# The tail of a two-layer graph network: edges in 171 pairs of tiles with a table of groups, against 90 units of four

## The chip, the cores and the metric

One core of one Trainium2 chip runs the whole program. The metric is the device time of one execution in microseconds. The kernel before took 3299.7 us (median of 3 runs, 3299.06 to 3302.92).

## The reference

1250 nodes with 768 features and 41250 edges (`src`, `dst`), each with one of 34 types. Two layers, each followed by a residual and a layer norm. The first is two attention convolutions and a projection. The second, which the change touches, is in short:

```python
seg = edge_type * n + dst
agg = segment_sum(x[src], seg); mean = agg / max(cnt, 1)
h1  = einsum('rni,rio->no', mean, W_rel) + x @ W_root + b_rgcn
out = segment_sum(h1 @ W_gcn, normalised over src, dst) + b_gcn
```

## The kernel before

**Edges.** The edges are sorted by destination into 10 groups ("buckets") of 128 nodes. One tile is 128 edges, one on each partition; a unit is UT = 4 tiles that belong to one group. UNITS = 90 units (ET = 360 tiles) hold any 41250 edges; places left over in a group's last unit are padding of weight 0. `dst_s`, `w_s` and `idx_y` have a column per tile: the destination in the group, the edge's weight 1/count and the row to gather. `unit_bucket` says which group a unit adds to.

**The relation products.** The kernel first multiplies by the weights, then gathers: for two halves of the output columns (CH = 384) and 17 pairs of relations each it runs steps of 35 products (seven combinations m1 to m7 of blocks, by five node tiles t; a product is nine f16 matmuls, lines 2501 to 2504). ACT evicts m1, m7, m6 and m3 (L1286), DVE adds m2, m5 and m4 (L1936), SP stores the rows to `y_half`. PE's order in a step is m1(0), m1(1), m7(0), m7(1), m6(0), m6(1), m2(0) and so on; m6(t) waits until ACT has copied m1(t). ACT's step begins with `used_high` for the weights of m4 (L1219), m1_out(0), `used_high` for m3, m1_out(1), m7_out(0), m7_out(1). While the second half's products run, the edges of the first half are aggregated beside them.

**The tail.** The edges of the second half are aggregated last, when all of `y_half` is stored. POOL gathers a tile at a time (`tail_gather`, L911, one indirect DMA of 128 rows of 384 floats), into 16 buffers, after `e_sum` says that the tile 16 before is used. DVE makes the weighted one-hot of each tile (`tail_onehot`, L1910, scalars straight from `dst_s` and `w_s`), PE multiplies it by the gathered rows (`tail_sum`, L2490, fp32, two records per tile) and sums the four tiles of a unit in one bank of PSUM; two banks take turns, and unit u waits until unit u-2 is added. DVE reads the unit's group into a register and adds the bank to that group's rows (`edge_add`, L1922). ACT copies the indices of the unit six ahead (`tail_index`, `next_index`, L1267) after unit u is summed. Beside the units run, in an order that is written out:
- units 0 to 37 (ROOT_UNITS): the 35 products of the root weight, one and a half per unit, done by unit 20; then ten tiles of `cT` (640 KB each, L765), one every 1.5 units from unit 21 on, three buffers; ACT takes the high half (`c_split`), DVE the rest (`c_rest`, L1980) two units later, and the load of tile c+3 waits for the rest of tile c;
- units 38 to 87: 25 pieces of the first half's graph product and of its product by W_gcn (L2735 to L2748), one piece after every second unit; units 88 and 89 have none.

When all units are added (`e_added`), the second half's graph product, the last product and the layer norm follow (`FINAL`), from there to the end of the program.

**Two earlier places.** At the start DVE works out the groups' units from their counts (L1592 to L1601, each operation waits for the one before it: `after`). Between the two attention layers DVE runs `spread_pads` (L1804) and then waits for the second layer.

```python
            def edge_add(q, i, m, c, roots=0):
                V, place, _ = unit(q, i, m, c)
                b = dve.value_load(unit_bucket[0:1, bass.ds(i * m + c, 1)], min_val=0, max_val=NT - 1)
                o = bass.ds(b * CH, CH)
                dve.wait_ge(e_sum, V * UT + 2 * UT)
                dve.wait_ge(e_added, V + 2)
```

Of the kernel before, what the change touches and what calls it, by code (L numbers as in the profile page):

```python
# [5 lines left out]
ALU = mybir.AluOpType  # L6
# [9 lines left out]
def cdiv(a, b):  # L16
    return -(-a // b)


def program(nc, x, src, dst, etype, norm_g, norm_b, W1, a_src1, a_dst1, b1, W2, a_src2, a_dst2, b2,  # L20
# [24 lines left out]
    CW = N + R  # L45
    TURN, EYES = 6, 2
# [7 lines left out]
    with ctx:  # L54
# [71 lines left out]
        rel_inv = src_s[:, 0:NT * R].rearrange("p (b r) -> p b r", r=R)  # L126
        epsc = sb("epsc", [P, 1], F32)
# [402 lines left out]
        REST = UNITS - ROOT_UNITS  # L530
        assert REST == 2 * len(PIECES) + 2

# [32 lines left out]
        def tail_slot(i, m, c, t):  # L565

            units = len(tail_rows) // UT
            assert m % units == 0 or isinstance(i, int)
            k = c % units * UT + t
            before = UNITS // 2 + W_USES[0] if k < 2 * UT else W_USES[1]  # L570
            return k, (g_loaded + tail_loaded)[k], i * (m // units) + (c // units + before + 1 + EYES_READ[k])
# [13 lines left out]
        def _(sp):  # L585
# [175 lines left out]
            for c in range(NT):  # L761
                sp.wait_ge(e_added, UNITS + CT_AT[c] + 2)
# [6 lines left out]
            sp.wait_ge(e_added, HALVES * UNITS + 2)  # L769
# [11 lines left out]
        def _(pool):  # L781
# [120 lines left out]
            def tail_gather(i, m, c):  # L902

                V = i * m + (c + (HALVES - 1) * UNITS)
                pool.wait_ge(idx_next, V + 1)
                for t in range(UT):
# [3 lines left out]
                    k, loaded, _ = tail_slot(i, m, c, t)  # L910
                    nc.gpsimd.indirect_dma_start(  # L911
                        out=tail_rows[k], out_offset=None, in_=y_dram[HALVES - 1],
                        in_offset=bass.IndirectOffsetOnAxis(ap=idx_now[:, c % IDXB, t:t + 1], axis=0)).then_inc(loaded, 16)
# [77 lines left out]
            with pool.Fori(0, UNITS // (2 * IDXB)) as i:  # L991
                for c in range(2 * IDXB):
                    tail_gather(i, 2 * IDXB, c)
            for c in range(UNITS // (2 * IDXB) * 2 * IDXB, UNITS):
                tail_gather(0, UNITS, c)
# [12 lines left out]
        def _(act):  # L1008
# [485 lines left out]
            def tail_index(i, m, c):  # L1494

                act.wait_ge(e_sum, i * (m * UT) + ((HALVES - 1) * UNITS + c + 2) * UT)
                next_index(i * m + (c + IDXB), c)

            for u in range(ROOT_UNITS):
                for m, t in root_slots(u):  # L1500
                    root_out(m, t)
                tail_index(0, UNITS, u)
                for m, t in root_slots(u - 1) if u else ():
                    if m == 3:
                        root_high(t)
                if u in CT_SPLIT:
                    c_split(CT_SPLIT.index(u))
            for m in range(len(PIECES)):
                for c in (ROOT_UNITS + 2 * m, ROOT_UNITS + 2 * m + 1):
                    if c + IDXB < UNITS:  # L1510
                        tail_index(0, UNITS, c)
                piece_out(m)
            for c in range(ROOT_UNITS + 2 * len(PIECES), UNITS - IDXB):
                tail_index(0, UNITS, c)

            act.wait_ge(e_added, HALVES * UNITS + 2)
# [10 lines left out]
        def _(dve):  # L1527
# [66 lines left out]
            fcnt, uend, ustart, base = (small[:, i * NT:(i + 1) * NT] for i in range(1, 5))  # L1594
            after(nc.vector.tensor_scalar(smalli[:, :], bank[6][:, NT:2 * NT], float(UE - 1), None, ALU.add))
# [206 lines left out]

            def spread_pads():
# [11 lines left out]
            spread_pads()  # L1815
            dve.wait_ge(s2_ready, NT)
# [87 lines left out]
            def tail_onehot(i, m, c):  # L1904

                V, place, _ = unit(HALVES - 1, i, m, c)
                for t in range(UT):
                    at = bass.ds((i * m + c) * UT + t, 1)
                    dve.wait_ge(e_sum, V * UT + (t + 1 + UT - 2 * UT))
                    nc.vector.tensor_scalar(tail_oh[place * UT + t], iota[:, 0:P], dst_s[:, at], w_s[:, at],  # L1910
                                            ALU.is_equal, ALU.mult).then_inc(e_oh, 1)

# [227 lines left out]
            def root_add(t, u):  # L2140
# [4 lines left out]
                dve.wait_ge(e_added, UNITS + u + 3)  # L2145
# [12 lines left out]
            tail_onehot(0, UNITS, 0)  # L2158
# [6 lines left out]
            for u in range(ROOT_UNITS):  # L2165
                tail_onehot(0, UNITS, u + 1)
                for m, t in root_slots(u):
                    root_out(m, t)
                edge_add(HALVES - 1, 0, UNITS, u, roots)
# [10 lines left out]
            first, last = ROOT_UNITS, HALVES - 1  # L2180
            with dve.Fori(0, REST // 2 - 1) as i:
                tail_onehot(i, 2, first + 1)
                edge_add(last, i, 2, first, roots)
                tail_onehot(i, 2, first + 2)
                edge_add(last, i, 2, first + 1, roots)
            tail_onehot(0, 2, UNITS - 1)
            edge_add(last, 0, 2, UNITS - 2, roots)
            edge_add(last, 0, 2, UNITS - 1, roots)

            dve.wait_ge(e_added, HALVES * UNITS + 2)  # L2190
# [18 lines left out]
        def _(pe):  # L2209
# [271 lines left out]
            def tail_sum(i, m, c):  # L2481

                V, place, _ = unit(HALVES - 1, i, m, c)
                acc = bank[SUMS + place][:, 0:CH]
                pe.wait_ge(e_added, V + 1)
                for t in range(UT):
                    k, loaded, uses = tail_slot(i, m, c, t)
                    pe.wait_ge(e_oh, (i * m + c) * UT + (t + 1))
                    pe.wait_ge(loaded, uses * 16)
                    nc.tensor.matmul(acc, tail_oh[place * UT + t], tail_rows[k], start=(t == 0), stop=(t == UT - 1))\  # L2490
                        .then_inc(e_sum, 1)
# [222 lines left out]
            for u in range(ROOT_UNITS):  # L2714
                for m, t in root_slots(u):
                    MAKE[m](STEPS - 1, t)
                tail_sum(0, UNITS, u)
# [35 lines left out]
            for m, (kind, j, cs) in enumerate(PIECES):  # L2753
                tail_sum(0, UNITS, ROOT_UNITS + 2 * m)
                tail_sum(0, UNITS, ROOT_UNITS + 2 * m + 1)
# [9 lines left out]
            for u in range(ROOT_UNITS + 2 * len(PIECES), UNITS):  # L2765
                tail_sum(0, UNITS, u)

            pe.wait_ge(e_added, HALVES * UNITS + 2)
# [36 lines left out]
```

## Time and profile before

| what | value |
|---|---|
| median of 3 runs | 3299.7 us |
| the profiled execution's own time | 3300.49 us |
| its span, first to last instruction | 3298.8 us |
| mean granted TensorE clock | 0.982 |
| the tail, first gather to last add | 2735.15 to 3201.13 us |
| what follows the tail | 97.7 us |

Times in the rows are in us from the start of the span. PE is TensorE's matmuls, PEld its weight loads, DVE VectorE, ACT ScalarE, POOL GpSimd, SP the engine that issues the loads and stores. "Idle before" is the time an engine stood still before an instruction, with the instruction that ended it; "issue" is waiting for nothing that the profile shows, the engine's own sequencer included. Matmuls overlap in the records, so their means are longer than their spacing.

### The profile page before, as it was taken

The page shows a single profiled execution, that of the slowest core. Times are in us where ns is not written, and L with a number is a line of the kernel's source. Part 1 is how long each engine was busy: PE and PEld are TensorE (multiplying, and loading weights), DVE is VectorE, ACT ScalarE, POOL GpSimd, SP SyncE. Part 2 cuts the span into 40 slices and gives each one's busy share as a digit, 9 for nine tenths or more (in the row PEclk, how much of TensorE's full clock was granted, in tenths as well). Part 3 has the DMA queues.
Part 4 walks back from the last instruction along what each step waited for, and adds up shares of the span by engine and source line. Part 5 has one row for each costly group of instructions (what it writes and reads, how often), then busy time and mean ns, then how long its engine had stood idle before and what let it go on. Part 6 is the DMA issues. An engine that isn't in the chain of part 4 may idle for free.

```text
span 3298.8 us, 59790 instructions
## 1 busy us (share of the span) xinstructions
PE 3128.9 (95%) x17442; PEld 1963.0 (60%) x17442; DVE 2259.3 (68%) x4621; ACT 1431.7 (43%) x2534; POOL 1822.0 (55%) x1510
## 2 busy tenths in 40 slices
PE   6979998988999999999999999999999999879998
PEld 4545558967566666666666666666666665434545
DVE  8989988959855564555646788787887865443335
ACT  3746647636534344343444554554555532110010
POOL 3767700001666666766514566566665636777763
PEclk9999999998999999999999999999999999999999
DMA  4047722021343333333325555565565634665542
GB/s 135 2 157 214 213 75 84 1 91 44 118 137 109 128 133 101 132 112 129 134 105 175 168 195 177 175 200 171 171 202 166 196 126 145 191 215 158 157 139 78
DMA packets 241012, 458.34 MB, mean 139 GB/s; under 512 B 40228, under 2 KB 180387, under 8 KB 240918
## 3 DMA queue, kind: packets, MB, share of 16 engines
q1 hardware_dynamic: 169248, 271.42, 23.7%
q0 software_dynamic: 71280, 185.21, 19.8%
q8 instruction: 54, 0.88, 0.1%
q10 hardware_dynamic: 390, 0.50, 0.1%
q14 instruction: 40, 0.33, 0.0%
HBM read 302.39 MB, written 154.52 MB: 139 GB/s over the span
## 4 chain that ended last, share of the span: by engine, by line
PE 78%; DVE 7%; POOL 5%; DMA 5%; issue 4%; ACT 2%; POOLq 0%; DVEq 0%; ACTq 0%
PE bank L2501 18%; PE bank L2503 18%; PE bank L2504 18%; PE bank L2490 4%; DMA arena<-y_half,idx_now 4%; PE bank L2290 3%; POOL placed_dram L808 3%; PE bank L2343 2%; PE bank L2284 2%; PE bank L2403 2%; PE bank L2478 2%; PE bank L2477 2%; DVE arena L1743 2%; DVE arena L1781 2%; PE bank L2748 2%
## 5 line engine op out<-in xcount | busy, mean ns | idle before, releaser
L2501 PE MATMUL bank<-arena 128*128 128x384 f16 x3675 | 1200.1, 327 | 1.2 <-ACT arena L1286 1.2
L2504 PE MATMUL bank<-arena 128*128 128x384 f16 x3675 | 1199.0, 326 | 0.0
L2503 PE MATMUL bank<-arena 128*128 128x384 f16 x3675 | 1199.0, 326 | 0.0
L1286 ACT ACTIVATE arena<-bank,winv 128x384 f32<-128x384 f32 x700 | 399.8, 578 | 836.1 <-PE bank L2504 834.7
L1936 DVE SCALAR_TENSOR_TENSOR arena<-bank,winv,arena 128x384 f32<-128x384 f32 x525 | 318.6, 614 | 382.0 <-PE bank L2504 378.5
L2501 PEld LDWEIGHTS bank<-arena 128*128 128x128 f16 x3675 | 359.7, 98 | 247.6 <-issue 14.9
L2504 PEld LDWEIGHTS bank<-arena 128*128 128x128 f16 x3675 | 359.6, 98 | 237.9 <-issue 0.5
L2503 PEld LDWEIGHTS bank<-arena 128*128 128x128 f16 x3675 | 360.1, 98 | 233.2 <-issue 5.2
L1860 DVE SCALAR_TENSOR_TENSOR arena<-arena,wscale 128x1152 f16<-128x1152 f32 x245 | 379.8, 1586 | 161.0 <-ACT arena L1219 153.4
L897 POOL DMA_INDIRECT arena<-y_half,idx_now x360 | 401.2, 1114 | 161.1 <-issue 99.5
L911 POOL DMA_INDIRECT arena<-y_half,idx_now x360 | 351.9, 977 | 116.8 <-issue 98.2
L2490 PE MATMUL bank<-arena 128*128 128x384 f32 x720 | 277.1, 516 | 61.3 <-DMA arena<-y_half,idx_now 47.0
L1922 DVE TENSOR_TENSOR arena<-arena,bank 128x384 f32 x180 | 99.3, 552 | 299.5 <-PE bank L2490 269.5
L1219 ACT ACTIVATE arena<-arena,wscale 128x1152 f16<-128x1152 f32 x245 | 294.6, 1245 | 1.6 <-DVE wscale L1847 1.5
L1261 ACT ACTIVATE agg_hi<-arena,typ_s 128x384 fp32r<-128x384 f32 x360 | 191.7, 606 | 197.0 <-PE bank L2478 196.5
L884 POOL DMA_INDIRECT w_now<-rel_inv_dram,idx_now x192 | 195.5, 1018 | 111.5 <-PE bank L2504 67.0
L2490 PEld LDWEIGHTS bank<-arena 128*128 128x128 f32 x720 | 130.7, 196 | 192.8 <-issue 92.3
L1901 DVE SCALAR_TENSOR_TENSOR agg_lo<-arena,typ_s,agg_hi 128x384 fp32r<-128x384 f32 x360 | 220.7, 613 | 15.6 <-ACT agg_hi L1261 15.6
L884 POOL DMA_INDIRECT w_odd<-rel_inv_dram,idx_odd x168 | 168.7, 1004 | 101.9 <-PE bank L2504 65.7
L863 POOL TENSOR_TENSOR arena<-arena 128x1152 f32<-128x1152 f32 x35 | 92.4, 2639 | 236.7 <-DVE arena L1860 236.4
L920 POOL MEMSET arena<- 1x1250 f32 x1 | 1.1, 1137 | 379.3 <-DVE arena L1766 379.3
L2403 PE MATMUL bank<-arena 128*128 128x193 f32 (+6 forms) x1200 | 187.4, 319 | 20.6 <-DVE arena L1781 19.3
(280 smaller groups left out, 4686.9 us busy)
## 6 DMA issues: line engine op xcount, KB each, us to landing
y_half<-arena SPq DMA_DIRECT2D x306, 384.0 KB
arena<-in_L_gnn_W_rel_dram SPq DMA_DIRECT2D x68, 1152.0 KB, 8.2
arena<-y_half,idx_now POOLq DMA_INDIRECT x720, 3.1
y_half<-arena SPq DMA_DIRECT2D x34, 294.0 KB
cT_dram<-arena SPq DMA_DIRECT2D x1, 5625.0 KB
arena<-cT_dram SPq DMA_DIRECT2D x9, 625.0 KB, 4.7
arena<-in_x_dram SPq DMA_DIRECT2D x10, 384.0 KB, 9.3
xu_dram<-arena SPq DMA_DIRECT2D x9, 384.0 KB, 2.3
```

The lines of the kernel that those rows point to most:

```text
L884: nc.gpsimd.indirect_dma_start(out=w_bufs[b][:, c, t:t + 1], out_offset=None, in_=w_dram, in_offset=bass.IndirectOffsetOnAxis(ap=idx_bufs[ ...
L897: nc.gpsimd.indirect_dma_start(out=graw[place * UT + t], out_offset=None, in_=y_dram[q], in_offset=bass.IndirectOffsetOnAxis(ap=idx_now[:, ...
L911: nc.gpsimd.indirect_dma_start(out=tail_rows[k], out_offset=None, in_=y_dram[HALVES - 1], in_offset=bass.IndirectOffsetOnAxis(ap=idx_now[: ...
L1219: nc.scalar.activation(by_rel(w_hi[m - 1]), block, ACT.Copy, scale=wscale[:, 0:1]).then_inc(w_hi_ready, 1)
L1286: nc.scalar.activation(y[half][:, :, c * CQ:(c + 1) * CQ], acc, ACT.Copy, scale=scale).then_inc(r_copied, 1)
L1860: nc.vector.scalar_tensor_tensor(by_rel(w_lo[m - 1]), block, wscale[:, 0:1], by_rel(w_hi[m - 1]), ALU.mult, ALU.subtract).then_inc(w_lo_re ...
L1936: nc.vector.scalar_tensor_tensor(to, acc, winv[:, 0:1], to, ALU.mult, ALU.add).then_inc(r_added, 1)
L2403: ins = nc.tensor.matmul(g.acc(b, r), ring[(h * NT + c) % 4][0:rc, b * P:b * P + r], g.h[0:rc, c, h, :], start=(c == 0 and b % g.per == 0) ...
L2490: nc.tensor.matmul(acc, tail_oh[place * UT + t], tail_rows[k], start=(t == 0), stop=(t == UT - 1))\
L2501: nc.tensor.matmul(acc, h, w_hi[m - 1][:, k, :], start=fresh and k == 0, stop=False, skip_group_check=True)
L2503: nc.tensor.matmul(acc, h, w_lo[m - 1][:, k, :], start=False, stop=False, skip_group_check=True)
L2504: ins = nc.tensor.matmul(acc, l, w_hi[m - 1][:, k, :], start=False, stop=k == KH - 1, skip_group_check=True)
```

## The change

Units are still four tiles wide for the buffers and indices, but the tail now works by pairs of tiles (PT = 2). A group takes as many pairs as its edges fill (at least one), so 171 pairs, 342 tiles, hold any 41250 edges, in TU = 86 units, the last with one pair. Where a group's pairs end inside one of its old units, the columns in between are skipped: `pair_table` makes, for each pair, the column of its first tile (`tail_col`) and its group (`tail_bucket`), over the space of `src_s`. ACT reads the column into a register and copies indices, weights and destinations of each pair (three copies of 128x2, where one of 128x4 stood for a unit). The first six units' copies stand ahead of the last step of relation products. DVE reads the group and adds once per pair; each pair has its own bank, and a pair waits for the add of the pair two before it. ROOT_UNITS is 34 instead of 38, and `cT` is loaded one tile per unit. The loops of POOL's and DVE's tail are written out.

```diff
+    PT = 2
+    PAIR_E = PT * P
+    PAIRED = (E + NT * PAIR_E - 1) // PAIR_E
+    TU = cdiv(PAIRED, UT // PT)
...
-        ROOT_UNITS, ROOTS = 38, 4
+        ROOT_UNITS, ROOTS = 34, 4
         CT_UNIT = 21
-        CT_AT = [CT_UNIT + 3 * c // 2 for c in range(NT)]
+        CT_AT = [CT_UNIT + c for c in range(NT)]
...
-        REST = UNITS - ROOT_UNITS
+        REST = TU - ROOT_UNITS
...
+            def tail_gather(u):
+
+                V = u + (HALVES - 1) * UNITS
+                pool.wait_ge(idx_next, V + IDXB + 1)
+                for t in range(len(pairs_of(u)) * PT):
                     if t % FREE == 0:
                         pool.wait_ge(e_sum, V * UT + (t + FREE + UT - len(tail_rows)))
                         pool.nop(nofuse=True)
...
+            for u in range(TU):
+                tail_gather(u)
...
+            def pairs_in(u):
+
+                for h in pairs_of(u):
+                    at = act.value_load(tail_col[0:1, u * (UT // PT) + h:u * (UT // PT) + h + 1], min_val=0, max_val=ET - PT)
+                    o, of = slice(h * PT, (h + 1) * PT), bass.ds(at, PT)
+                    nc.scalar.copy(idx_now[:, u % IDXB, o], idx_y[:, of])
+                    nc.scalar.copy(w_now[:, u % IDXB, o], w_s[:, of])
+                    ins = nc.scalar.copy(w_odd[:, u % IDXB, o], dst_s[:, of])
+                ins.then_inc(idx_next, 1)
...
+            act.wait_ge(e_sum, UNITS * UT + UT)
+            act.wait_ge(idx_next, UNITS + IDXB)
+            for u in range(IDXB):
+                pairs_in(u)
             one_step(1, PAIRS - 1, HALVES, 0, None)
...
+            after(nc.vector.tensor_copy(small[:, 5 * NT:6 * NT], bank[6][:, NT:2 * NT]))
...
+            def pair_table():
+
+                ucount, held, first, ends, more = (small[:, i * NT:(i + 1) * NT] for i in (1, 5, 6, 7, 4))
+                after(nc.vector.tensor_scalar(smalli[:, :], held, float(PAIR_E - 1), None, ALU.add))
+                after(nc.vector.tensor_scalar(smalli[:, :], smalli[:, :], PAIR_E.bit_length() - 1, None, ALU.arith_shift_right))
+                after(nc.vector.tensor_scalar(first, smalli[:, :], 1.0, None, ALU.max))
+                after(nc.vector.tensor_tensor_scan(ends, ones[:, 0:NT], first, 0.0, ALU.mult, ALU.add))
+                after(nc.vector.scalar_tensor_tensor(more, ucount, float(UT // PT), first, ALU.mult, ALU.subtract))
+                dve.wait_ge(rel_inv_stored, 48)
+                col, to = src_s[:, 0:PAIRED], src_s[:, PAIRED:2 * PAIRED]
+                j, gap = iota[:, 0:PAIRED], typ_s[:, 0:PAIRED]
+                after(nc.vector.tensor_copy(col, j))
+                after(nc.vector.tensor_scalar(to, j, ends[:, 0:1], None, ALU.is_ge))
+                for k in range(NT - 1):
+                    if k:
+                        after(nc.vector.scalar_tensor_tensor(to, j, ends[:, k:k + 1], to, ALU.is_ge, ALU.add))
+                    after(nc.vector.tensor_scalar(gap, j, ends[:, k:k + 1], more[:, k:k + 1], ALU.is_ge, ALU.mult))
+                    after(nc.vector.tensor_tensor(col, col, gap, ALU.add))
+                after(nc.vector.tensor_scalar(tail_col, col, float(PT), None, ALU.mult))
+                after(nc.vector.tensor_copy(tail_bucket, to))
...
             spread_pads()
+            pair_table()
             dve.wait_ge(s2_ready, NT)
...
+                    nc.vector.tensor_scalar(tail_oh[u % 2 * UT + t], iota[:, 0:P], w_odd[:, u % IDXB, at], w_now[:, u % IDXB, at],
                                             ALU.is_equal, ALU.mult).then_inc(e_oh, 1)
+
+            def tail_add(u, roots):
+
+                V = u + (HALVES - 1) * UNITS
+                for h in pairs_of(u):
+                    j = u * (UT // PT) + h
+                    b = dve.value_load(tail_bucket[0:1, j:j + 1], min_val=0, max_val=NT - 1)
+                    o = bass.ds(b * CH, CH)
+                    dve.wait_ge(e_sum, V * UT + (UT + (h + 1) * PT))
+                    dve.wait_ge(e_added, UNITS + j + 2)
+                    if roots:
+                        dve.wait_ge(root_added, roots)
+                    nc.vector.tensor_tensor(hs_flat[HALVES - 1][:, o], hs_flat[HALVES - 1][:, o], bank[SUMS + h][:, 0:CH],
+                                            ALU.add).then_inc(e_added, 1)
...
+            def tail_sum(u):
+
+                for h in pairs_of(u):
+                    acc = bank[SUMS + h][:, 0:CH]
+                    pe.wait_ge(e_added, UNITS + (u * (UT // PT) + h + 1))
+                    for t in range(h * PT, (h + 1) * PT):
+                        k, loaded, uses = tail_slot(u, t)
+                        pe.wait_ge(e_oh, u * UT + (t + 1))
+                        pe.wait_ge(loaded, uses * 16)
+                        nc.tensor.matmul(acc, tail_oh[u % 2 * UT + t], tail_rows[k], start=(t % PT == 0),
+                                         stop=(t % PT == PT - 1)).then_inc(e_sum, 1)
```

## Rows read from the trace of the kernel before

**Rows 1.** The page: busy time and share of the span, and the ending chain by engine.
```profile
PE 3128.9 (95%) x17442; PEld 1963.0 (60%) x17442; DVE 2259.3 (68%) x4621; ACT 1431.7 (43%) x2534; POOL 1822.0 (55%) x1510
...
PE 78%; DVE 7%; POOL 5%; DMA 5%; issue 4%; ACT 2%; POOLq 0%; DVEq 0%; ACTq 0%
```

**Rows 2.** Busy time by stretch of the tail; then clock, DMA share, GB/s.
```profile
core 0: us, PE busy (x) PEld busy (x) DVE busy (x) ACT busy (x) POOL busy (x), PEclk, DMA share, GB/s
...
2885.00:2935.00 50.00, 33.22 (x73) 15.21 (x74) 22.48 (x51) 8.55 (x15) 38.42 (x39) 0.83 0.78 255
2985.00:3035.00 50.00, 45.20 (x156) 21.05 (x155) 16.41 (x50) 2.91 (x11) 38.03 (x40) 1.00 0.55 157
3135.00:3185.00 50.00, 47.54 (x142) 25.78 (x141) 16.30 (x50) 6.80 (x18) 37.81 (x41) 1.00 0.56 157
```

**Rows 3.** The tail's gathers, line 911: durations, what ended POOL's idle time.
```profile
L911 POOL DMA_INDIRECT arena<-y_half,idx_now x360: 942/946/2831, 2735.2 to 3195.5; - x180
...
  issue: 98.2, 299
  PE bank L2490: 18.6, 61
```

**Rows 4.** Timeline of POOL: start, duration, instruction, idle before it.
```profile
2831.41 0.95 POOL L911 DMA_INDIRECT arena<-y_half,idx_now  x1 [0.30 <-PE bank L2490]
2832.66 1.28 POOL L911 DMA_INDIRECT arena<-y_half,idx_now  x1 [0.30 <-issue]
...
3195.48 0.95 POOL L911 DMA_INDIRECT arena<-y_half,idx_now  x1 [0.30 <-issue]
```

**Rows 5.** The chain that ended last, at the end of the tail.
```profile
3191.37 3.87 PE bank L2748 x12
3195.24 5.17 PE bank L2490 x16
...
3200.56 0.57 DVE arena L1922
```

**Rows 6.** The last relation step's beginning on ACT, timeline.
```profile
2679.07 0.58 ACT L1286 ACTIVATE arena<-bank,winv 128x384 f32<-128x384 f32 x1 [2.10 <-PE bank L2504]
2679.55 1.24 ACT L1219 ACTIVATE arena<-arena,wscale 128x1152 f16<-128x1152 f32 x1
2680.69 0.57 ACT L1286 ACTIVATE arena<-bank,winv 128x384 f32<-128x384 f32 x1
...
2683.46 0.58 ACT L1286 ACTIVATE arena<-bank,winv 128x384 f32<-128x384 f32 x1 [0.58 <-PE bank L2504]
2684.92 0.58 ACT L1286 ACTIVATE arena<-bank,winv 128x384 f32<-128x384 f32 x1 [0.88 <-PE bank L2504]
```

**Rows 7.** Six index copies in a row, timeline of ACT; line 1267's register work.
```profile
1728.85 0.66 ACT L1267 COPY idx_now<-idx_y 128x4 int32<-128x4 int32 x6
...
L1267 ACTq FUSED_REGOPS  x90: 65/65/65, 1780.8 to 2664.6; - x90
```

**Rows 8.** Adds behind a register load, line 1922: idle by releaser; two of them, timeline.
```profile
  issue: 30.1, 60
...
2500.29 0.55 DVE L1922 TENSOR_TENSOR arena<-arena,bank 128x384 f32 x1 [1.03 <-issue]
...
2513.48 0.55 DVE L1922 TENSOR_TENSOR arena<-arena,bank 128x384 f32 x1 [0.22 <-issue]
```

**Rows 9.** Timeline of DVE: at the start, and between the attention layers.
```profile
42.27 0.17 DVE L1597 TENSOR_SCALAR small<-smalli 128x10 f32<-128x10 int32 x1
...
664.71 0.53 DVE L1809 SCALAR_TENSOR_TENSOR idx_y<-typ_s,idx_y 128x360 int32<-128x360 f32 x1
...
697.90 1.46 DVE L1720 CUSTOM_DVE_ANT_0 arena<-arena 128x1250 f32<-128x1250 f32 x1 [32.44 <-ACT arena L1079]
```

**Rows 10.** Timeline of DVE in the tail's steady part; the rest of cT, line 1980.
```profile
3055.85 1.11 DVE L1910 TENSOR_SCALAR arena<-iota,dst_s,typ_s 128x128 f32<-128x128 f16 x4
...
L1980 DVE TENSOR_TENSOR arena<-arena x10: 1452/1454/1476, 2869.3 to 2939.6; 128x1250 f16<-128x1250 f32 x9, 98x1250 f16<-98x1250 f32 x1
```

More of the change, by code:

```diff
@@ L126, in program @@
         rel_inv = src_s[:, 0:NT * R].rearrange("p (b r) -> p b r", r=R)
+        tail_col, tail_bucket = (src_s[:, i * PAIRED:(i + 1) * PAIRED].bitcast(I32) for i in range(2))
+        assert 2 * PAIRED <= ET
         epsc = sb("epsc", [P, 1], F32)
@@ L563, in unit, with tail_slot @@
             return i * m + (c + q * UNITS), c % 2, i * (m // 2) + (c // 2 + q * (UNITS // 2) + W_USES[0])
-        def tail_slot(i, m, c, t):
+        def tail_slot(u, t):
             units = len(tail_rows) // UT
-            assert m % units == 0 or isinstance(i, int)
-            k = c % units * UT + t
+            k = u % units * UT + t
             before = UNITS // 2 + W_USES[0] if k < 2 * UT else W_USES[1]
-            return k, (g_loaded + tail_loaded)[k], i * (m // units) + (c // units + before + 1 + EYES_READ[k])
+            return k, (g_loaded + tail_loaded)[k], u // units + before + 1 + EYES_READ[k]
         class Count:
@@ L990, in _ @@
             pool.wait_ge(e_lo, UNITS * UT + 2 * UT)
[L991 to L995, printed above, removed]
+            for u in range(TU):
+                tail_gather(u)
             pool.wait_ge(row_loaded, 48)
@@ L1509, in _ @@
                 for c in (ROOT_UNITS + 2 * m, ROOT_UNITS + 2 * m + 1):
-                    if c + IDXB < UNITS:
-                        tail_index(0, UNITS, c)
+                    if c + IDXB < TU:
+                        tail_index(c)
                 piece_out(m)
-            for c in range(ROOT_UNITS + 2 * len(PIECES), UNITS - IDXB):
-                tail_index(0, UNITS, c)
-            act.wait_ge(e_added, HALVES * UNITS + 2)
+            act.wait_ge(e_added, UNITS + PAIRED + 2)
             for n in range(NT):
@@ L1902, in edge_low, with tail_onehot @@
                                                    agg_hi[:, t, :].bitcast(F32), ALU.mult, ALU.subtract).then_inc(e_lo, 1)
[L1904 to L1908, printed above, removed]
+            def tail_onehot(u):
+                V = u + (HALVES - 1) * UNITS
+                dve.wait_ge(idx_next, V + IDXB + 1)
+                for t in range(len(pairs_of(u)) * PT):
+                    at = slice(t, t + 1)
                     dve.wait_ge(e_sum, V * UT + (t + 1 + UT - 2 * UT))
-                    nc.vector.tensor_scalar(tail_oh[place * UT + t], iota[:, 0:P], dst_s[:, at], w_s[:, at],
+                    nc.vector.tensor_scalar(tail_oh[u % 2 * UT + t], iota[:, 0:P], w_odd[:, u % IDXB, at], w_now[:, u % IDXB, at],
                                             ALU.is_equal, ALU.mult).then_inc(e_oh, 1)
+            def tail_add(u, roots):
+                V = u + (HALVES - 1) * UNITS
+                for h in pairs_of(u):
[8 more added lines that the diff above has]
+                                            ALU.add).then_inc(e_added, 1)
             def edge_add(q, i, m, c, roots=0):
@@ L2165, in _ @@
             for u in range(ROOT_UNITS):
-                tail_onehot(0, UNITS, u + 1)
+                tail_onehot(u + 1)
                 for m, t in root_slots(u):
                     root_out(m, t)
-                edge_add(HALVES - 1, 0, UNITS, u, roots)
+                tail_add(u, roots)
                 for m, t in root_slots(u):
@@ L2179, in _ @@
                     c_rest(CT_SPLIT.index(u - 2))
[L2180 to L2190, printed above, removed]
+            for u in range(ROOT_UNITS, TU):
+                if u + 1 < TU:
+                    tail_onehot(u + 1)
+                tail_add(u, roots)
+            dve.wait_ge(e_added, UNITS + PAIRED + 2)
             dve.wait_ge(uT_psum, len(SUM_GROUPS))
@@ L2479, in edge_sum @@
                         .then_inc(e_sum, 1)
[L2481 to L2491, printed above, removed]
+            def tail_sum(u):
[8 more added lines that the diff above has]
+                                         stop=(t % PT == PT - 1)).then_inc(e_sum, 1)
             def product(s, m, t):
@@ L2764, in _ @@
                     times_wg(0, j, 3).then_inc(share_psum, 1)
-            for u in range(ROOT_UNITS + 2 * len(PIECES), UNITS):
-                tail_sum(0, UNITS, u)
-            pe.wait_ge(e_added, HALVES * UNITS + 2)
+            for u in range(ROOT_UNITS + 2 * len(PIECES), TU):
+                tail_sum(u)
+            pe.wait_ge(e_added, UNITS + PAIRED + 2)
             pe.wait_ge(share_ready, NT)
```

32 lines of the change are left out of this document (15 added, 17 removed).

## The prediction

> **What bounds the kernel now.** I read the page first: PE is busy 95% of the span and is 78% of the ending chain [rows 1]. That is an average over stages, so the question is what paces the stretch that the change touches, 2735.15 to 3201.13 us. The busy times by stretch say it is POOL: in the steady part 40 or 41 gathers fall into every 50 us, at full and at lowered clock alike, while PE's work differs from stretch to stretch and DVE has 16 us of 50 [rows 2]. The gathers' line says how: 942 ns at least, 946 in the middle, and the idle time between them ends by issue (98.2 us) or, 0.3 us each, by PE (18.6 us over 61) [rows 3]. So POOL never really waits for a free buffer. The timeline shows the beat, 2832.66 - 2831.41 = 1.25 us, of which 0.30 is the gap [rows 4]. All of it: 3195.48 - 2735.2 = 460.3 us for 359 beats, 1.282 each; 359 x 1.25 = 448.8, the other 11.5 us are gathers that ran long. After the last gather starts, its landing, PE's last sums and DVE's add take 3201.13 - 3195.48 = 5.65 us [rows 5]; then comes the work that needs all units, 97.7 us, which the change leaves alone. The tail's length therefore passes into the time one to one.
>
> **The tail's gathers.** 360 become 342. 18 x 1.25 = **22.5 us less**. I take the plain beat, since the long gathers (1.28 at 2832.66) stand beside DVE's work on roots and rows, which stays. At the mean of 1.282 it would be 23.1. Against it: `cT` now comes in every 5.0 us instead of 7.5, 640 KB each, so the DMA load there rises from 157 + 85 = 242 GB/s to 157 + 128 = 285 (255 measured in that stretch, at a DMA share of 0.78 [rows 2]). POOL still made 39 gathers in that stretch, so one lost beat per 50 us, twice, is my bound: 0 to 2.5 us lost, taken as 0. The load of tile c+3 starts after unit 24+c and is wanted by the last of its readers three units later, 15 us; it holds nobody up.
>
> **PE's end.** PE leaves the last piece at 3195.24 with 8 tiles to sum, 5.17 us, 0.65 each [rows 5]. With 6 tiles left after the last piece it has 3.9. Where PE is late at the end, that is up to 1.3 us more; where the last landing counts, nothing. I take 0 and keep it for the range.
>
> **ACT's block ahead of the last relation step.** This is the price. Between m3_out of the step before (2679.07) and `used_high` (2679.55) ACT has no idle time [rows 6], and there it gets 12 pairs, each a register load and three copies. The copies: 0.66 us for six, 0.11 each, 0.33 a pair [rows 7]. The register arithmetic of a moving address: 65 ns, three times, 0.20 [rows 7]. The load itself is in no row; the nearest are DVE's adds behind one, 30.1 / 60 = 0.50 us of idle time each, from 0.22 to 1.03 [rows 8]. With 0.50: 12 x (0.50 + 0.33 + 0.20) = 12.4 us. From below, 12 x (0.22 + 0.33) = 6.6 (the arithmetic hidden); from above, 12 x 1.56 = 18.7. What covers it: m1_out(0) ends at 2680.69 + 0.57 = 2681.26, and PE wants it for m6(0), which starts when m7(1) is through, 2684.9 (ACT's eviction of it starts there). Cover 3.6 us. The copy of m1(1) has about the same. The rest moves PE, then the stores, then the first gather, which waits for them: 12.4 - 3.6 = **8.8 us more**, from 3.0 to 15.1. The two waits put before the block are met by then: the last edge sum of the half stands ahead of m4(4) and m3(4) on PE, and ACT has just evicted m3(4). Queued behind the block are only the step's evictions and DVE's low halves for m4 and m3; PE wants the low half of m4 six products (8.8 us) after m6(0) begins, so those are not late next.
>
> That register load has a price in the Trainium skill, DMA: Bandwidth & Descriptors, Latency and other measured facts: a `tensor_load` takes some 600 ns at least. By it the block would be 12 x (0.60 + 0.53) = 13.6 us and the loss 10.0, an estimate; no row here shows that load by itself.
>
> **ACT and DVE in the tail.** ACT per unit: 2 x 1.03 = 2.1 us instead of one copy. It is six units ahead (30 us), so no gather waits; ACT is busy 3 to 9 us of 50 [rows 2]. The cover is gone only if ACT falls two units back. DVE per unit: 4 one-hots 1.11 [rows 10], two adds 1.10, two loads 1.0, 3.2 of 5.0 us; with a piece of `cT` (1.45) 4.7, still under 5.0. Behind DVE's new wait for the indices stand the one-hots; ACT wrote these indices five units before. All at nothing, covered by POOL's beat.
>
> **PE in the tail.** A pair waits for the add two pairs back, where a unit waited for the add two units back. The other pair's sum, 2 x 0.65 = 1.3 us, lies between; from PE's end (3195.24 + 5.17 = 3200.41) to the add's end (3201.13) it takes 0.72 us [rows 5]. It fits; nothing. PE's work per two units with a piece is 5.17 + 3.87 = 9.0 of 10.0 us.
>
> **The table.** 5 operations of 10 columns and 30 of 171, each waiting for the one before. From above, every one as dear as 0.53 us for 360 columns [rows 9] and 0.04 between: 35 x 0.57 = 20 us. DVE idles 32.4 us there, until 697.90 [rows 9]. Nothing. The copy of the counts at the start is in a chain where each operation waits: 0.17 + 0.04 = **0.2 us more**.
>
> **The sum.** 3300.49 - 22.5 + 8.8 + 0.2 = 3287.0. The profiled execution is 0.8 us above the median of 3299.7, which I leave in the range and round to **3286.5**. Dropping POOL's and DVE's loops costs nothing that I see; PE's and ACT's tails are written out already.
>
> **Rivals.**
> - The block is nearly hidden: the sequencer loads registers while copies run. Then 3.0 or less is lost, 3279 to 3281. For it: the 0.22 in [rows 8]; against: these copies are too short to hide a load behind.
> - The block is at its upper end, or PE's gap there lowers its clock. The clock fell to 0.83 where PE was busy 33 of 50 us [rows 2]. 15.1 instead of 8.8 gives 3293; a few us at half clock more, 3296.
> - Slower: PE and DVE become a loop that paces the piece stretch. If DVE's load of the group is not ahead of the sum, a pair costs 1.3 + 0.72 with no overlap, a unit 4.0, with half a piece (1.9) 6.0 against 5.0. Over 50 units 1.0 x 50 = 50 us: 3337. It decides from 13.5 / 50 = 0.27 us per unit on. For it: DVE's idle of up to 1.03 behind a load; against: the load stands ahead of the wait, and PE's next pair goes to the other bank.
> - The added adds (81) lengthen gathers as the 1.28 did, by 0.33 each: 27 us lost, 3313. Against: in the steady stretch 10 adds stand beside 41 gathers of 0.92 us on average, 37.81 / 41 [rows 2]; an add reads PSUM and one operand of SBUF.
> - That it doesn't do what it says can be left out: 342 gathers are written out, whatever the edges are.
>
> **Chances.** Forecast, 3282 to 3291: 0.60. Block hidden: 0.14. Block dear or clock: 0.16. Loop or adds, wholly or in part: 0.10, half of it beyond the old time. The range is 3278 to 3296: it takes in the block's bounds, 3281.2 to 3293.3, with PE's 1.3 below and the `cT` bound of 2.5 above. 0.2% is 6.6 us, about what a measurement of this kernel can tell from no change; faster than 3293.1: 0.82, within: 0.12, slower than 3306.3: 0.06.
>
> **What would show it.** Right: 342 gathers at a spacing of 1.25; ACT's idle-free block of 36 copies ahead of `used_high` with a span near 12 us; PE idle about 9 us before m6(0) of that step; the tail from first gather to last add 443 us instead of 466; nothing changed before 2679 but 0.2 us. Wrong: POOL idle by PE or ACT for more than 0.3 us at a time (the loop, or late indices), gathers over 1.0 us in the steady stretch, or DVE's first operation of the second attention layer not waiting for ACT any more.

## The result: 1.8% slower, and the profile after

The changed kernel takes **3361.8 us** (median of 4 runs, 3355.1 to 3363.6), the kernel before, run beside it, 3301.3 (4 runs, 3299.1 to 3303.8): a ratio of 1.0179, interval 1.0167 to 1.0191. 3286.5 was forecast. The profiled execution has a span of 3353.4 us against 3298.8, 54.6 us more, at a mean granted clock of 0.976.

Cut the two spans at the gathers, whose first and last start the view of a line gives, and the 54.6 us fall into place (starts before; after):

| stretch | before | after | difference |
|---|---|---|---|
| start to the first gather of the first half's edges | 1732.9 | 1729.2 | -3.7 |
| from there to that line's last gather: 15 passes of a loop | 921.3 | 993.9 | **+72.6** |
| to the tail's first gather | 81.0 | 88.7 | +7.7 |
| the tail, first to last gather | 460.3 | 438.9 | **-21.4** |
| last gather to the end | 103.3 | 102.7 | -0.6 |

So the tail did what it was changed for. The loss is in a stretch that the change doesn't touch, two relation steps to a pass, in which the first half's edges are aggregated beside the products.

The page of the kernel after: busy times, the queues that carry instructions, the ending chain by engine (beside [rows 1]), and the two groups of gathers (the first is the stretch before the tail, the second the tail):

```profile
PE 3142.2 (94%) x17406; PEld 1959.7 (58%) x17406; DVE 2292.4 (68%) x4720; ACT 1487.5 (44%) x2963; POOL 1816.1 (54%) x1492
...
q14 instruction: 133, 1.09, 0.1%
...
PE 73%; DVE 8%; issue 7%; DMA 5%; POOL 5%; ACT 2%; DVEq 1%; ACTq 0%; SPq 0%; POOLq 0%
...
L907 POOL DMA_INDIRECT arena<-y_half,idx_now x360 | 410.3, 1140 | 243.7 <-DVE agg_lo L1943 134.3
...
L921 POOL DMA_INDIRECT arena<-y_half,idx_now x342 | 336.0, 982 | 111.6 <-issue 91.5
```

PE's share of the chain fell from 78% to 73% and "issue" rose from 4% to 7%. The line of queue 14 gives packets, MB and share: 133 packets of instructions. The same two lines of the kernel before:

```profile
q14 instruction: 40, 0.33, 0.0%
...
L897 POOL DMA_INDIRECT arena<-y_half,idx_now x360 | 401.2, 1114 | 161.1 <-issue 99.5
```

40 packets there, and POOL's idle time was 83 us shorter. Who makes it wait after the change is in the waits of the stretch 1785 to 2740 us (us in total, times, longest):

```profile
POOL arena L907 <- DVE agg_lo L1943: 133.6, 27, 7.6
DVE agg_oh L1941 <- issue: 65.9, 14, 5.1
PEld bank L2529 <- DVE agg_lo L1943: 56.1, 56, 2.2
PE bank L2529 <- DVE agg_lo L1943: 38.9, 28, 1.8
...
DVE agg_lo L1943 <- issue: 16.5, 14, 1.3
```

and of the kernel before, 1785 to 2680 us, where neither PE nor DVE's `agg_oh` has such a line:

```profile
POOL arena L897 <- DVE agg_lo L1901: 56.5, 27, 2.8
```

DVE stands still by "issue" 14 times for 4.7 us and 14 times for 1.2. The timeline of DVE (start, duration, instruction, idle before) shows where one of each lies, at the head of a pass:

```profile
2553.36 0.56 DVE L1979 TENSOR_TENSOR arena<-arena,bank 128x384 f32 x1 [1.04 <-issue]
2558.70 0.29 DVE L1941 TENSOR_SCALAR agg_oh<-iota,dst_s 128x128 fp32r<-128x128 f16 x1 [4.79 <-issue]
...
2561.03 0.62 DVE L1943 SCALAR_TENSOR_TENSOR agg_lo<-arena,typ_s,agg_hi 128x384 fp32r<-128x384 f32 x1 [1.31 <-issue]
```

`edge_add` (now L1979) is the last instruction of a pass, `agg_oh` the first of the next. Before the change the same pair stands at 2500.29 [rows 8] and 2500.93, with no idle time between. Nothing that another engine does ends the 4.79 us as far as the profile shows, which leaves DVE's own sequencer. 14 is the number of times that a loop of 15 passes goes back to its start. The 82.4 us of both kinds turn into 72.6 on the path, since PE, which paces these steps, waits for `agg_lo` behind them.

The tail itself, by stretches as in [rows 2], one with `cT` being loaded and two steady ones:

```profile
core 0: us, PE busy (x) PEld busy (x) DVE busy (x) ACT busy (x) POOL busy (x), PEclk, DMA share, GB/s
...
2961.00:3011.00 50.00, 33.77 (x83) 15.12 (x82) 29.38 (x64) 13.62 (x60) 39.34 (x36) 0.86 0.75 245
3061.00:3111.00 50.00, 45.32 (x156) 20.96 (x155) 21.88 (x60) 8.76 (x62) 37.80 (x41) 1.00 0.55 158
3191.00:3241.00 50.00, 47.42 (x142) 25.65 (x141) 21.25 (x60) 10.94 (x55) 37.82 (x41) 1.00 0.56 158
```

41 gathers in 50 us beside 20 adds, where 10 stood: 0.92 us of POOL each (37.80 / 41), as before. The stretch in which `cT` is loaded has 36 gathers, against 39 in the one of before, and gathers there take 39.34 / 36 = 1.09 us. And the tail's gathers by themselves:

```profile
L921 POOL DMA_INDIRECT arena<-y_half,idx_now x342: 942/946/2835, 2811.8 to 3250.7; - x171
...
  issue: 91.5, 276
  PE bank L2542: 13.1, 43
  ACT w_odd L1283: 7.0, 23
```

POOL still waits for nothing: the idle time named PE or ACT is 0.3 us each, the gap that every gather has.

### The profile page after: what moved, and what is told of

The parts are those of the page before. It is cut to its first block, busy times and chain, and to the rows that moved or that the text cites. A ratio compares the mean times of both kernels' runs of the same rounds, so it can differ in the third digit from the quotient of the medians.

```text
span 3353.4 us, 60900 instructions
## 1 busy us (share of the span) xinstructions
PE 3142.2 (94%) x17406; PEld 1959.7 (58%) x17406; DVE 2292.4 (68%) x4720; ACT 1487.5 (44%) x2963; POOL 1816.1 (54%) x1492
## 3 DMA queue, kind: packets, MB, share of 16 engines
q14 instruction: 133, 1.09, 0.1%
## 4 chain that ended last, share of the span: by engine, by line
PE 73%; DVE 8%; issue 7%; DMA 5%; POOL 5%; ACT 2%; DVEq 1%; ACTq 0%; SPq 0%; POOLq 0%
PE bank L2553 16%; PE bank L2555 16%; PE bank L2556 16%; PE bank L2542 4%; DMA arena<-y_half,idx_now 4%; PE bank L2342 4%; POOL placed_dram L818 3%; PE bank L2395 2%; PE bank L2336 2%; PE bank L2529 2%; PE bank L2455 2%; DVE arena L1763 2%; PE bank L2530 2%; PE bank L2800 2%; DVE arena L1801 2%
## 5 line engine op out<-in xcount | busy, mean ns | idle before, releaser
L2542 PE MATMUL bank<-arena 128*128 128x384 f32 x684 | 262.7, 515 | 53.3 <-DMA arena<-y_half,idx_now 43.4
```

Of the source, the lines that this page charges most:

```text
L2542: nc.tensor.matmul(acc, tail_oh[u % 2 * UT + t], tail_rows[k], start=(t % PT == 0), stop=(t % PT == PT - 1)).then_inc(e_sum, 1)
```

## The experiments

### What is to be explained, and by what

The stretch of +72.6 us has the same instructions on all engines as before. What lies ahead of it is different: `pair_table` and the copied counts put 37 more instructions ahead of DVE's loop (counted in the built programs, register instructions included: the loop is 279 instructions long, with 1300 instructions ahead of it before and 1337 after; the loops of PE, ACT and POOL did not move).

- **Theory, place.** DVE's instructions are fetched in blocks. Where the loop lies across one block more than fit, each jump back to its start must fetch again. It depends on the loop's place alone: any 37 small instructions ahead of it would do it, and some more would undo it. The Trainium skill, Advanced Engine Details and Errata, ISA Cache, has such blocks: lines of 256 instructions, of which an engine keeps two; and Runtime: NRT & Kernel Launch, Instruction fetch mechanics, says that a taken branch to outside the present window forces a fetch. From this figure of the Trainium skill one can estimate that a loop of 279 touches three lines only where it begins in one of the last 22 places of a line (256 + 23 = 279).
- **Rival, table.** What the table does (its operations, the space of `src_s` overwritten, the registers) slows the passes.
- **Rival, length.** The program as a whole is longer (DVE 2328 instructions before, 3373 after, counted), with its tail written out; the fetching suffers wherever the extra instructions stand.

The padding used is one `memset` of a place that nobody reads, waited for like the rest of that chain (0.124 us each: 61 take 7.57 us below), in DVE's long wait between the attention layers. The first four kernels ran together on one chip, beside 22 runs of the kernel before (median 3301.0).

### The kernel after with 24 more instructions ahead of the loop

```diff
             pair_table()
+            for _ in range(24):
+                after(nc.vector.memset(credit[:, 7:8], 0.0))
             dve.wait_ge(s2_ready, NT)
```

> The changed kernel with 24 tiny memsets (0.2 us each) put behind pair_table, in DVE's idle time between the attention layers. All that is moved is the place of DVE's later code, by 24 instructions. Theory 1 (place): the steps of relation products beside which the first half's edges are added run 4.8 us longer per pass, because DVE's loop of 279 instructions, which the change pushed 37 instructions further on, now lies so that it is fetched again in each of its 15 passes (the traces: 4.79 us and 1.31 us of DVE waiting for 'issue' at the head of each pass, and 133 packets on the queue of instructions instead of 40). 24 more instructions bring it over the bad place: 3290 us (3362 less 72), 40 to 50 packets on that queue, no such idle time. Theory 2 (length): it is the longer program as such (written-out tail, table): 3362 us. Theory 3 (the table or its data slow the loop, or contention): 3362 us.

Measured: 3291.8 us (7 runs, 3288.8 to 3293.3), ratio 0.9973, interval 0.9961 to 0.9984; span 3287.0. Adding work took 70.0 us off the changed kernel (whose own runs stood beside a kernel before at 3301.3, here 3301.0), and with the place put right the change is faster than before by 9.2 us, 0.3%. Its packets of instructions are 63, more than the 40 to 50 expected. Its page, and its waits of `agg_lo` from 1785 to 2760 us; no line of DVE by "issue" is left there:

```profile
q14 instruction: 63, 0.52, 0.1%
```

```profile
POOL arena L907 <- DVE agg_lo L1945: 53.3, 26, 2.8
...
PE bank L2531 <- DVE agg_lo L1945: 0.7, 1, 0.7
```

By the cuts of the first table the stretches are 1729.0, 924.2 (+2.9 against before), 89.8 (+8.8), 441.4 (-18.9) and 102.6: the loss in the passes is gone, everything else of the change is still there.

### The kernel before with 37 instructions ahead of its loop

```diff
             spread_pads()
+            for _ in range(37):
+                after(nc.vector.memset(credit[:, 7:8], 0.0))
             dve.wait_ge(s2_ready, NT)
```

> The kernel before with 37 tiny memsets behind spread_pads, so that DVE's loop stands where it stands in the changed kernel. Nothing else of the change is in it. Theory 1 (place): 3300 + 72 = 3372 us, with the same idle times at the head of each pass and about 130 packets of instructions. Theories 2 and 3 (length as such, the table, contention): 3300 us; 37 instructions of 2328 are nothing.

Measured: 3375.3 us (4 runs, 3373.4 to 3376.0), ratio 1.0223, interval 1.0206 to 1.0240. Nothing of the table or of the tail is in this kernel, and it loses 74.3 us, with 110 packets where about 130 were expected. Its page; its waits from 1785 to 2760 us; a head of a pass on DVE:

```profile
q14 instruction: 110, 0.90, 0.1%
```

```profile
POOL arena L897 <- DVE agg_lo L1903: 136.3, 27, 7.9
DVE agg_oh L1901 <- issue: 68.4, 14, 5.1
...
DVE agg_lo L1903 <- issue: 17.3, 14, 1.4
```

```profile
2564.94 0.29 DVE L1901 TENSOR_SCALAR agg_oh<-iota,dst_s 128x128 fp32r<-128x128 f16 x1 [5.05 <-issue]
```

The same 14 stops, of the same length, at the same instructions, and 110 - 40 = 70 packets of instructions more, 5 per stop, of (0.90 - 0.33) MB / 70 = 8.1 KB each. In the changed kernel it is 133 - 63 = 70 too. The rival of the table falls.

### The kernel before with 61, and with 36 behind the loop

61 is 37 + 24, so the loop stands where it does in the changed kernel with 24 more. The diff is the one above with 61 for 37.

> The kernel before with 61 tiny memsets at the same place. Theory 1 (place): over the bad place, 3300 us again, though it is longer than the one with 37. A rival that every instruction ahead of the loop costs: 3300 + 72 x 61 / 37 = 3419 us.

Measured: 3304.2 us (8 runs, 3297.3 to 3307.7), ratio 1.0013, interval 1.0002 to 1.0023. That is 3.2 us above the kernel before, just clear of no change, and neither the 74 of the 37 nor the 118 of the rival. The memsets and what DVE waits for behind them, by its timeline, and the page:

```profile
665.09 7.57 DVE L1817 MEMSET credit<- 128x1 f32 x61
695.81 1.46 DVE L1720 CUSTOM_DVE_ANT_0 arena<-arena 128x1250 f32<-128x1250 f32 x1 [23.15 <-ACT arena L1079]
```

```profile
q14 instruction: 41, 0.34, 0.0%
```

23.15 us of DVE's idle time [rows 9] are still left, so the padding is hidden.

The other kernel has the instructions behind DVE's loop, four with each of nine units of the tail:

```diff
+                if 24 <= u < 33:
+                    for _ in range(4):
+                        after(nc.vector.memset(credit[:, 7:8], 0.0))
```

> The kernel before with 36 tiny memsets behind the loop, four in each of units 24 to 32 of the tail, where DVE has time. Theory 1 (place): the loop is not moved, 3300 us. Theory 2 (a longer program as such): as with 37 ahead of it.

Measured: 3298.7 us (8 runs, 3296.4 to 3302.8), ratio 0.9995, interval 0.9984 to 1.0005, 40 packets. A program that is 36 instructions longer behind the loop costs nothing here. The rival of the length falls for this form of it; that the written-out tail itself costs nothing is shown by the kernel with 24.

### Where the bad places end, and whether they return after 256

Four kernels, of one run each, two beside runs of the kernel before at 3413.1 us (13 runs, 3410.6 to 3421.4) and two at 3399.3 (19 runs, 3394.8 to 3405.1). These were other chips, about 100 us slower with every kernel; each time is compared with the kernel before on its own chip. The diff is the one above with 26, 48, 256 and 293.

> The kernel before with 26 memsets ahead of the loop instead of 37 (bad) or 61 (good). The Trainium skill (Advanced Engine Details and Errata, ISA Cache) says that the instruction memory of such an engine has two lines of 256 instructions. If a loop of 279 costs nothing while it touches two lines and is fetched anew when it touches three, the bad places are a stretch of 22 or 23 in every 256, so of 26 and 48, which lie 22 apart around the bad 37, at most one is bad (3372 us, some 130 packets of instructions), the other is 3300 us with some 40. Rival: the bad stretch is wide (a cost that grows as the loop moves): both bad, or both in between (3330 to 3350).

> The kernel before with 48 memsets ahead of the loop. By the theory of two lines: if 26 is bad this one is good, 3300 us, and at most one of the two is bad; both good is possible too. Rival of a wide bad stretch: 3372 us for both, or something in between.

> The kernel before with 256 memsets behind spread_pads (0.124 us each, 31.8 us, against 30.7 us of idle time there: about 1 us). By lines of 256 instructions the loop is where it was before, modulo a line: 3302 us and some 45 packets of instructions. Rival, that the place counts in another way (another period, an absolute place): anything between 3302 and 3375.

> The kernel before with 293 = 256 + 37 memsets (36.3 us, about 6 us beyond the idle time). By lines of 256 this is the bad place again: 3301 + 6 + 74 = 3381 us and some 115 packets. By an absolute place or another period: 3307 us.

| added ahead of the loop | time, us | against before | packets |
|---|---|---|---|
| 26 | 3480.4 | +67.4 | 110 |
| 48 | 3410.3 | -2.8 | 41 |
| 256 | 3399.8 | +0.6 | 42 |
| 293 = 256 + 37 | 3479.1 | +79.8 | 112 |

The waits of the kernel with 26 and then of the one with 293, 1780 to 2860 us:

```profile
DVE agg_oh L1901 <- issue: 87.4, 15, 6.3
```

```profile
DVE agg_oh L1901 <- issue: 68.2, 14, 5.1
```

With 293 the stops are those of 37. With 26 they are of one kind only: fourteen of 6.1 to 6.4 us at `agg_oh` (the fifteenth is 0.34, at the start of the loop), and `agg_lo` has no line by "issue"; the packets are the same 110. So the place also moves the second stop.

0, 48, 61 and 256 are good places, 26, 37 and 293 bad ones. Adding 256 to a good and to a bad place changed neither, and the run of bad places, if it is one run, is at least 12 and at most 47 wide, which holds the 22 estimated above; a smooth cost of length, an absolute place or a single unlucky place is excluded. That 256 is the period itself is not shown: 128 or 64 would give the same seven answers, as nothing between 61 and 256 was run. One run each is enough for a difference of 67 us or more beside 13 and 19 runs that lie within 11. Which places exactly are bad was not tried, nor does the count in the built program tell where a block begins on the chip: by it the loop would begin at places 46 and 57 of 256 (1326 and 1337), not in the last 22. Either a fixed number of instructions that the count doesn't have stands ahead, or the estimate of 22 is not the whole of it; that blocks are fetched anew is shown by the packets and the stops, their size and number are not.

### The block on ACT, split in two

The second term of the prediction is the block of 12 pairs ahead of the last relation step. In this kernel, which has the 24 memsets too, six pairs stand behind `m6_out(1)` of that step and six behind `m6_out(3)`, in ACT's idle time:

```diff
+                for u in range(IDXB // 2 if first_pairs else 0):
+                    pairs_in(u)
...
+                for u in range(IDXB // 2, IDXB if first_pairs else 0):
+                    pairs_in(u)
...
-            for u in range(IDXB):
-                pairs_in(u)
-            one_step(1, PAIRS - 1, HALVES, 0, None)
+            one_step(1, PAIRS - 1, HALVES, 0, None, first_pairs=True)
```

> The changed kernel with the 24 memsets and with ACT's first twelve pairs of the tail taken from ahead of the last relation step into it: six behind m6_out(1), six behind m6_out(3), where ACT waits some 9.7 us for PE. Theory A (the block is on the path: PE stood 7.2 us at m6(0) of that step in the changed kernel's trace): 3291.8 - 7.2 = 3284.6 us, and PE has no gap there. Theory B (PE's gap is hidden later, by POOL's beat or the stores): no change, 3292 us. If six pairs (4.9 us) do not fit their place, m3_out(0) is late and up to 1 us comes back.

Measured: 3403.5 us (9 runs, 3399.3 to 3409.2) against 3413.1, ratio 0.9971, interval 0.9961 to 0.9981. It beats the kernel before, but on this chip the unsplit one had not run, so the pair was run again together:

> The changed kernel with 24 memsets, as in the first experiment, beside the next one on the same chip (the run of the split block stood on a chip on which the kernel before itself took 3413 us, POOL's gathers having gaps of 2.65 us there, so the two could not be compared). Ratio to before 0.997.

> As the run of the split block before. Theory A (ACT's block is on the path): 7.2 us less than its neighbour with the block in one piece, ratio to before 0.995. Theory B (hidden later): the same as its neighbour.

Unsplit 3398.0 us (11 runs, 3393.6 to 3404.3), ratio 0.9996, interval 0.9987 to 1.0005; split 3390.5 (9 runs, 3387.0 to 3396.7), ratio 0.9973, interval 0.9963 to 0.9983. Both ratios miss what was expected (0.997 and 0.995): on this chip the kernel with 24 is not clear of no change, for which see the next section. The difference of the two came as expected: the split is worth 7.5 us, give or take some 3 by the spread of these runs, and its first gather of the tail starts at 2762.3 instead of 2771.5. PE's timeline of the unsplit one has this, and the split one has no such idle time in that step:

```profile
2719.07 0.48 PE L2555 MATMUL bank<-arena 128*128 128x384 f16 x1 [7.19 <-ACT arena L1303]
```

ACT's timeline of the split one shows the first copy of the first and of the sixth pair, in what was idle time, and the eviction behind them, which still waits for PE:

```profile
2715.35 0.19 ACT L1281 COPY idx_now<-idx_y 128x2 int32 x1
...
2719.66 0.19 ACT L1281 COPY idx_now<-idx_y 128x2 int32 x1 [0.42 <-issue]
...
2724.95 0.58 ACT L1303 ACTIVATE arena<-bank,winv 128x384 f32<-128x384 f32 x1 [4.91 <-PE bank L2560]
```

It was run once more on a fourth chip:

> The version with DVE's loop at a good place and ACT's block split, once more: on a chip where the kernel before takes 3301 us it should take 3291.8 - 7.4 = 3284 us, ratio 0.995, because there the tail's gathers keep their spacing of 1.25 us; on one where the gathers have gaps (before 3399 to 3413 us) the ratio stays at 0.997.

3391.0 us (7 runs, 3387.2 to 3396.3) against 3400.1 (12 runs), ratio 0.9974, interval 0.9963 to 0.9985. On all three of these chips this version is 8.8 to 9.6 us below the kernel before. On the first chip it did not run; the kernel with 24 alone is at 3291.8 there, and taking 7.5 from it would give 3284, which is an estimate.

### What the slower chips do to the tail

With 24 the change won 9.2 us on the first chip and 1.3 on the second to run it. The gathers of the tail, first to last, take 515.7 us there against 523.6 in the kernel before (with 256 memsets, the one of its kind profiled there with its loop at a good place): 7.9 us less, not 18.9 or 21.4. POOL's timeline of the kernel with 24 on that chip, two of the gaps that are not 0.3 us:

```profile
2850.16 0.95 POOL L921 DMA_INDIRECT arena<-y_half,idx_now  x1 [1.26 <-issue]
...
2862.38 0.95 POOL L921 DMA_INDIRECT arena<-y_half,idx_now  x1 [2.49 <-issue]
```

They return about every 12.2 us (2874.61, 2886.86, 2899.10, 2911.28), and 342 gathers have 161.1 us of idle time by "issue" instead of 93.5. The kernel before with 256 has gaps on that chip too, longer and half as often, about every 23.5 us in its steady part ("remote" is the view's name for what ended them):

```profile
3063.84 0.95 POOL L911 DMA_INDIRECT arena<-y_half,idx_now  x1 [3.69 <-remote]
...
3087.39 0.94 POOL L911 DMA_INDIRECT arena<-y_half,idx_now  x1 [3.72 <-remote]
```

So a gather takes 523.6 / 359 = 1.458 us there before the change and 515.7 / 341 = 1.512 after it. The 18 gathers are worth 26.3 us at that beat, but each of those that stay has become 0.054 us dearer, which takes 18.4 back. This holds in every profile from these chips: 1.458 to 1.491 in four of the kernel before with memsets, 1.508 to 1.538 in four with the new tail. On the first chip the beat grew by 0.005 to 0.012 only (1.282 to 1.287 and 1.294). What makes these gaps, why the new tail has more of them, and whether they are of the same kind as DVE's stops, was not tried.

## Why the prediction was wrong

**The step that failed** is the table's, with the line under the sum. "Nothing", it says of 35 operations hidden in DVE's idle 32.4 us, and "dropping POOL's and DVE's loops costs nothing that I see" (which held on the first chip, by the kernel with 24); and then "nothing changed before 2679 but 0.2 us". The duration of the table was priced, and rightly: it ran from 665.3 to about 678 and DVE still waited 18.07 us for ACT behind it. Its number of instructions was not priced. 37 of them ahead of a loop of 279 moved that loop to a place where each of 14 returns stops DVE for 4.7 and 1.2 us, 72.6 us in the profiled execution and 70.0 by the kernel with 24. No rival of the prediction had this: all of them looked for the loss inside the tail or at the block. The slower rival came nearest in size (50 us), by luck, with a mechanism that did not occur. Of the three signs given for being wrong none appeared; what failed was a sign of being right, "nothing changed before 2679 but 0.2 us".

Could it have been seen? The trace of before shows a loop with no such stop and 40 packets of instructions, so nothing in it warns. The program does: the length of a loop, and that the change puts instructions ahead of it.

**The gathers** were nearly right: 22.5 us forecast, 21.4 measured, and 18.9 in the profile of the kernel with 24, which has the same tail. The mean beat is 438.9 / 341 = 1.287 us (1.282 before; 1.294 with 24), POOL waits for nobody, and the spacing in the steady part is still 1.25. Of the 1.1 and 3.6 us missing only the first is inside the bound of 0 to 2.5 given for `cT`, and only as a net sum. The gathers alone, by stretches of 50 us, the densest stretch of `cT` and the one behind it:

```profile
core 0: us, POOL busy (x), PEclk, DMA share, GB/s
...
2951.00:3001.00 50.00, 39.64 (x35) 0.83 0.78 260
3001.00:3051.00 50.00, 37.81 (x41) 1.00 0.56 156
```

At 260 GB/s instead of 255 the densest stretch has 35 gathers, four fewer than 39, where one lost beat was my bound. The stretch ahead of it has 39, as each of the two had before (38.42 us each). The stretches behind have 41 where three had 40 before, so most of it comes back; why they do is not shown. Loading `cT` more densely was taken at nothing and costs up to 4 x 1.25 = 5 us where it happens. The prediction also has 40 or 41 gathers in a stretch at lowered clock; its own row shows 39.

**The block on ACT** was right in kind and a little too dear. The timeline of ACT after, the first copy of the first, of the eleventh and of the twelfth pair, then what stands behind:

```profile
2746.53 0.58 ACT L1303 ACTIVATE arena<-bank,winv 128x384 f32<-128x384 f32 x1 [2.10 <-PE bank L2556]
2747.37 0.19 ACT L1281 COPY idx_now<-idx_y 128x2 int32 x1 [0.26 <-issue]
...
2756.57 0.19 ACT L1281 COPY idx_now<-idx_y 128x2 int32 x1 [0.42 <-issue]
...
2757.37 0.19 ACT L1281 COPY idx_now<-idx_y 128x2 int32 x1 [0.42 <-issue]
2757.47 0.19 ACT L1282 COPY w_now<-typ_s 128x2 f32 x1
...
2757.65 1.25 ACT L1226 ACTIVATE arena<-arena,wscale 128x1152 f16<-128x1152 f32 x1
```

A pair takes 2757.37 - 2756.57 = 0.80 us, not 1.03: three copies issue 0.10 apart, and from the third's issue (2756.76) to the next pair's first it is 0.61, load and arithmetic together, where 0.11 + 0.50 + 0.20 = 0.81 were taken. (The 600 ns that the Trainium skill, DMA: Bandwidth & Descriptors, Latency and other measured facts, gives for a `tensor_load` agree with the 0.61 if the arithmetic is hidden in it.) In [rows 6] `used_high` starts 0.48 us after the eviction (2679.55 - 2679.07); here that would be 2747.01, and it starts at 2757.65: the block costs ACT 10.6 us instead of 12.4. PE's timeline:

```profile
2759.52 0.48 PE L2553 MATMUL bank<-arena 128*128 128x384 f16 x1 [7.18 <-ACT arena L1303]
```

7.2 us instead of 8.8, so the cover was 3.4 where 3.6 was worked out; the stretch grew by 7.7. The split kernel shows the same by an edit, 7.5 us.

**Costed at nothing, and nothing:** ACT's copies in the tail (23 gathers by 0.3 us, which is the gap that each has), the adds (gathers of 0.92 us beside 20 of them), the loop of PE and DVE (not seen: DVE has 21 of 50 us), PE's end (last gather to the end 102.7 against 103.3). The 0.2 us of the counts is too small to find in a stretch that came out 3.7 shorter. These 3.7 need not be the change's: the kernel before has its first such gather at 1732.9, with 61 memsets at 1729.0.

**The sum of the stretches as measured, without the passes:** 3300.5 - 21.4 + 7.7 - 3.7 - 0.6 = 3282.5, and 72.6 on top give the 3355.1 us of the profiled execution. With the place put right by the 24 the kernel takes 3291.8, 5.3 above the forecast and inside its range; beside its own kernel before it wins 9.2 us of the 13.2 forecast (3299.7 - 3286.5). On the slower chip where it ran it wins 1.3, and neither the forecast nor its range says anything of that.

## What to carry to other kernels

Count what a change adds or removes ahead of a loop, not only what it costs to run: this loop of 279 instructions ran free or paid some 5 us per return, by its place alone. In the profile it shows as idle time by "issue" at the head of each pass and as packets on the queue that carries instructions (40 against 110 here); try a few dozen tiny instructions in an idle stretch ahead of the loop before judging such a change. A change that looks worse by a per cent or two in a part that it doesn't touch may be good: here 24 idle instructions turned +1.8% into -0.3%.

## What was not expected of the hardware

- Instructions ahead of a loop changed its time by 67 to 80 us over 14 returns, about 5.3 us per return on the first chip (74.3 / 14), and 256 more instructions changed nothing in a good place nor in a bad one.
- 24 memsets of one column made a kernel 70.0 us faster.
- A copy of 128x2 on ACT takes 0.19 us, yet such copies start 0.10 us apart; with a register load between two of them it is 0.61 us, 0.42 of it idle.
- The same kernels take 3% more on other chips, there with gaps on POOL in the tail: about 3.7 us every 23.5 us before the change, about 2.5 us every 12.2 us after it, so that 18 gathers fewer won 7.9 us instead of some 20. Their cause is open.
